# Plain float32 products in place of rounded high and low pairs, in the ternary and the last integer network

## The reference, cut to what matters

```
ternary:  a = silu((x @ w1.T) * w1_s) * ((x @ w2.T) * w2_s)      # 128 -> 512
          b = gelu((a @ h1.T) * h1_s)                            # 512 -> 512
          c = gelu((b @ h2.T) * h2_s)                            # 512 -> 512
          y = (c @ w3.T) * w3_s                                  # 512 -> 128
          with w1, w2, h1, h2, w3 in {-1, 0, 1}
integer:  y = (silu(x @ gate.T / 127) * (x @ up.T / 127)) @ down.T / 127   # 128 -> 384 -> 128
```

## Time and profile before

| what | value |
| --- | --- |
| median of 3 runs | 1074.12 us (1063.49 to 1074.72) |
| profiled execution, first to last instruction | 1068.8 us |
| PE busy | 941.6 us, 88% |
| DVE busy | 786.1 us, 74% |
| ACT busy | 692.7 us, 65% |
| POOL busy | 583.4 us, 55% |
| mean granted clock of TensorE | 0.893 of full speed |

### The profile page before, as it was taken

How to read it: one execution, slowest core, us unless ns; L and a number is a source line. 1 busy time by engine, 2 the same in 40 slices (tenths; PEclk the granted TensorE clock), 3 DMA queues, 4 the chain that set the end, 5 groups by cost and what they waited for, 6 DMA issues and landing times. The chain is left out here.

```text
span 1068.8 us, 19776 instructions
## 1 busy us (share of the span) xinstructions
PE 941.6 (88%) x6850; PEld 690.5 (65%) x6850; DVE 786.1 (74%) x1468; ACT 692.7 (65%) x1920; POOL 583.4 (55%) x622
## 2 busy tenths in 40 slices
PE   8999999999999977787889988888988897897786
PEld 5888868676767336556656666666767676576544
DVE  4888875757466788987895898797698979733346
ACT  5767655555564476694695678786687776656454
POOL 0111044333333777777777667777777777776001
PEclk9999999999999678997795689897798978989899
DMA  7100001000000563533522423331331333131001
GB/s 237 40 21 2 2 1 45 1 1 1 1 1 12 124 146 92 132 81 80 130 59 61 101 61 73 73 70 41 73 73 38 73 73 74 47 105 40 1 1 39
DMA packets 58737, 62.07 MB, mean 58 GB/s; under 512 B 27760, under 2 KB 43152, under 8 KB 58256
## 3 DMA queue, kind: packets, MB, share of 16 engines
q1 hardware_dynamic: 42768, 36.41, 13.2%
q0 software_dynamic: 15872, 24.41, 10.1%
HBM read 52.65 MB, written 8.13 MB: 57 GB/s over the span
## 5 line engine op out<-in xcount | busy, mean ns | idle before, releaser
L791 POOL DMA_INDIRECT gathered_rows<-key_table,idx_T x496 | 482.5, 973 | 157.6 <-issue 146.6
L2382 DVE TENSOR_TENSOR turned_rows<-bank,rank_rope 96x512 f32<-96x512 f32 x128 | 87.3, 682 | 83.3 <-PE bank L1293 82.1
L1293 PE MATMUL bank<-ident,gathered_rows 128*96 128x128 f32 x512 | 92.6, 311 | 11.8 <-DVE turned_rows L2382 7.1
L2356 DVE SCALAR_TENSOR_TENSOR index_sums<-index_relu,iw,index_sums 128x512 f32<-128x512 f32 (+4 forms) x114 | 75.4, 661 | 33.4 <-ACT index_relu L1826 30.8
L832 PE MATMUL bank<-index_k_hi,index_q 128*128 128x512 f32 (+5 forms) x160 | 77.2, 485 | 19.3 <-DVE idx_T L2376 11.6
L1826 ACT ACTIVATE index_relu<-bank 128x512 f32<-128x512 f32 (+4 forms) x152 | 75.1, 507 | 24.0 <-PE bank L832 23.6
L1848 ACT ACTIVATE probs<-masked_scores,attn_columns 128x208 f32<-128x208 f32 x128 | 59.5, 465 | 31.3 <-DVE attn_columns L2392 26.7
L832 PE MATMUL bank<-probs_window,local_values 80*32 80x128 f32 x256 | 57.4, 311 | 24.7 <-ACT probs_picked L1864 23.1
L1293 PEld LDWEIGHTS bank<-ident,gathered_rows 128*96 128x96 f32 x512 | 66.0, 144 | 20.5 <-issue 11.4
L2364 DVE MAX8 top<-index_sums 128x8 f32<-128x320 f32 (+13 forms) x56 | 75.8, 1354 | 1.0
L2366 DVE FIND_INDEX8 idx_u<-top,index_sums 128x8 uint32<-128x320 f32 (+13 forms) x56 | 75.5, 1348 | 0.0
(11 more groups left out here) (295 smaller groups left out, 2430.4 us busy)
## 6 DMA issues: line engine op xcount, KB each, us to landing
queries_in<-q_rot SPq DMA_DIRECT2D x32, 256.0 KB
gathered_rows<-key_table,idx_T POOLq DMA_INDIRECT x496, 2.5
q_rot<-rotated SPq DMA_DIRECT2D x16, 256.0 KB, 3.3
queries_in<-q_lat SPq DMA_DIRECT2D x16, 256.0 KB
h<-in_h SPq DMA_DIRECT2D x2, 1024.0 KB, 7.9
q_lat<-q_latent_sb SPq DMA_DIRECT2D x8, 256.0 KB
local_values<-key_table SPq DMA_DIRECT2D x15, 80.0 KB
rope_tables<-in_cos_ql SPq DMA_DIRECT2D x4, 256.0 KB
```

Source lines behind the costliest of these rows:

```text
L791: pool.indirect_dma_start(out=G[i % 2][:, gather_place(i, q), :], out_offset=None, in_=key_table[0:index_width(i), :], in_offset=bass.Indi ...
L1293: last = pe.transpose(bank[2][0:ROW, j * P:(j + 1) * P], G[i % 2][:, gather_place(i, 4 * g + j), :], ident[:])
L2356: v.scalar_tensor_tensor(s_, r_, iw[:, h:h + 1], s_, ALU.mult, ALU.add).then_inc(i_used, 1)
L2382: v.tensor_tensor(GT[n % 2].rearrange("r (j p) -> r j p", j=4), bank[2][0:ROW, :].rearrange("r (j p) -> r j p", j=4), rank_rope[:].unsquee ...
```

## The change

Weights and activations of the three networks stay float32, and each product is one plain float32 product. The casts (POOL, ACT), the subtractions (DVE), the rounding of the weights on POOL and all semaphores for them go. ACT writes gelu, and DVE the gated product, directly into what the next product reads. The ternary weights are loaded where their rounded copies were. POOL has no work in the ternary networks any more: after its part of the first attention it goes on to the gathers, and all 16 of the first tile's come as soon as its indices are ready. SyncE no longer waits for the rounding before it loads the attention's weights, nor for the down products before the fixed rows of the first tile. In the last network the units take three pairs of banks in turn, (4, 5), (6, 7), (2, 3); unit 2 waits for the last variance to be read (`ln_sd`), unit j for the gated product of unit j - 3.

```diff
-        w1r, w2r, w3r = over("w1r", [HID], F32R), over("w2r", [HID], F32R), over("w3r", [NM, P], F32R)
-        h1r, h2r = over("h1r", [NM, HID], F32R), over("h2r", [NM, HID], F32R)
+        for n, shape in (("w1", [HID]), ("w2", [HID]), ("w3", [NM, P]), ("h1", [NM, HID]), ("h2", [NM, HID])):
+            LOAD[n] = over(n, shape)
...
+        def unit_banks(j):
+            at_ = (4, 6, 2)[j % 3]
+            return bank[at_], bank[at_ + 1]
...
 sync
-            sp.wait_ge(f_w, 5)
             for n, dst in (("WuqT", WuqT), ("WukT", WukT), ("WuvT", WuvT), ("Wout", Wout)):
...
             sp.wait_ge(t_store_k, STORES_K)
-            sp.wait_ge(f_down, 8)
...
 gpsimd
-                round_weights(2, (w1r, w1), (w2r, w2))
-                round_weights(3, (h1r, h1))
...
-            x_round(0)
-            for R in range(4):
-                ffn_half(R)
...
             def gather(i):
                 pool.wait_ge(i_idx, i + 1)
+                if i == 0:
+                    pool.wait_ge(t_store_k, STORES_K)
                 if i == 1:
                     pool.wait_ge(f_hid, 64)
-                for q in range(FIXED // QD + 4 * NM - EARLY_GATHER if i == 0 else 0, P // QD):
+                for q in range(FIXED // QD if i == 0 else 0, P // QD):
...
 tensor, ffn_up
-                    pe.wait_ge(f_x, 2 * R + u + 1)
+                    pe.wait_ge(ln_applied, LN0 + norm_index(k, r) + u + 1)
...
-                for o_, w in ((bank[2 * (j % 2)], w1r), (bank[2 * (j % 2) + 1], w2r)):
-                    mm(o_, w[:, m * P:m * P + P], x_hi[:, u, :], True, False)
-                    last = mm(o_, w[:, m * P:m * P + P], x_lo[:, u, :], False, True)
+                for o_, w in ((bank[2 * (j % 2)], w1), (bank[2 * (j % 2) + 1], w2)):
+                    last = mm(o_, w[:, m * P:m * P + P], chunk(xn, 2 * r + u))
...
 tensor, ffn_down
-                    pe.wait_ge(f_lo, 16 * R + 8 + u * NM + kk + 1)
-                    mm(bank[6 + u], w3r[:, kk, :], a_hi[:, u * NM + kk, :], kk == 0, False)
-                    last = mm(bank[6 + u], w3r[:, kk, :], a_lo[:, u * NM + kk, :], False, kk == NM - 1)
+                    pe.wait_ge(f_gelu, 16 * R + 8 + u * NM + kk + 1)
+                    last = mm(bank[6 + u], w3[:, kk, :], f_c[:, u * NM + kk, :], kk == 0, kk == NM - 1)
...
 tensor, hidden steps
-                        mm(bank[m], wt, hi[:, u * NM + kk, :], kk == 0, False)
-                        last = mm(bank[m], wt, lo[:, u * NM + kk, :], False, kk == NM - 1)
+                        last = mm(bank[m], w[:, kk, m * P:m * P + P], from_[:, u * NM + kk, :], kk == 0, kk == NM - 1)
...
 tensor, last network, unit
+                    elif j == 2:
+                        pe.wait_ge(ln_sd, LNF + NCH)
                     else:
-                        pe.wait_ge(n_gated, j - 1)
+                        pe.wait_ge(n_gated, j - 2)
...
-                    for o_, w in ((bank[4 + 2 * (j % 2)], gate_w), (bank[5 + 2 * (j % 2)], up_w)):
-                        mm(o_, w[:, m * P:m * P + P], x_hi[:, c % 2, :], True, False)
-                        last = mm(o_, w[:, m * P:m * P + P], x_lo[:, c % 2, :], False, True)
+                    for o_, w in zip(unit_banks(j), (gate_f, up_f)):
+                        last = mm(o_, w[:, m * P:m * P + P], chunk(xn, c))
...
 scalar
-                    if q >= 4:
-                        act.wait_ge(f_lo, 16 * R + q - 3)
-                    else:
-                        act.wait_ge(f_a, 8 * R + 5 + m)
-                    fn(f_full[:, q % 4, :], bank[m], ACT.Gelu, scale=sc[:, m:m + 1]).then_inc(f_gelu, 1)
+                    fn((f_b, f_c)[q // 8][:, q % 8, :], bank[m], ACT.Gelu, scale=sc[:, m:m + 1]).then_inc(f_gelu, 1)
...
 vector
-                    dve.wait_ge(f_gelu_hi, 16 * R + q + 1)
-                    v.tensor_tensor(lo[:, q % 8, :], f_full[:, q % 4, :], hi[:, q % 8, :], ALU.subtract).then_inc(f_lo, 1)
```

More of the change, by code:

```diff
@@ L173, in hybrid_kernel @@
         early_offset = (nc.sbuf_base + 31) // 32 * 32
-        h1, h2, w1, w2, w3, Wgk1, Wgk2 = (load(n) for n in ("h1", "h2", "w1", "w2", "w3", "Wgk1", "Wgk2"))
-        early_rest = sb("early_rest", [P, 2 * P])
+        early_rest = sb("early_rest", [P, 3 * T - 2 * P])
+        Wgk1, Wgk2 = load("Wgk1"), load("Wgk2")
         assert nc.sbuf_base - early_offset == 4 * 3 * T
@@ L235, in hybrid_kernel @@
         at[0] = LAYER
[L237 to L240, removed]
+        last_gated = over("last_gated", [2 * NM2, C])
+        at[0] = LAYER + P // QD * ROW
+        f_a, f_c, f_b = (over("ffn_" + n, [2 * NM, C]) for n in ("gated", "second", "first"))
+        SILU_AT = LAYER + 36 * C
+        at[0] = SILU_AT
         f_silu_sb, f_full = over("ffn_silu_out", [2, C]), over("ffn_full", [4, C])
@@ L389, in hybrid_kernel @@
                 "squared", "mean_sq", "rms", "rms_columns", "rms_turned", "normed", "projected_out"))
[L391 to L394, removed]
+        f_up, f_silu, f_gated, f_hid, f_gelu, f_down = (
+            sem("ffn_" + n) for n in ("up", "silu", "gated", "hidden", "gelu", "down"))
         ss_a, ss_u, ss_x, ss_y = (sem("ssm_" + n) for n in ("decay_ready", "inputs", "states", "outputs"))
@@ L426, in hybrid_kernel @@
                 "keys_x_values_added"))
-        (n_w, n_x_hi, n_x, n_up, n_silu, n_gated, n_gated_hi, n_a, n_down) = (
-            sem("int_" + n) for n in ("weights_ready", "x_hi", "x_split", "up", "silu", "gated", "gated_hi",
-                                      "gated_split", "down"))
+        n_w, n_up, n_silu, n_gated, n_down = (
+            sem("int_" + n) for n in ("weights_ready", "up", "silu", "gated", "down"))
         stored = sem("stored")
@@ L723, in gla @@
             def gla():
[L725 to L728, removed]
                 def out_gate(c):
@@ L752, in _ @@
             gla()
[L754 to L787, removed]
             def gather_rows(i, q):
@@ L1080, in ffn_half @@
                     stage, u, m = q // 8, q // 4 % 2, q % 4
-                    w, hi, lo = ((h1r, a_hi, a_lo), (h2r, b_hi, b_lo))[stage]
+                    w, from_ = ((h1, f_a), (h2, f_b))[stage]
                     if q < 4:
@@ L2008, in last_stages @@
                         act.wait_ge(n_gated, j - 1)
-                    fn(f_silu_sb[:, j % 2, :], bank[4 + 2 * (j % 2)], ACT.Silu, scale=INT_SCALE).then_inc(n_silu, 1)
-                    if j >= 1:
-                        gated_round(j - 1)
-                gated_round(NCH * NM2 - 1)
+                    fn(f_silu_sb[:, j % 2, :], unit_banks(j)[0], ACT.Silu, scale=INT_SCALE).then_inc(n_silu, 1)
             gla()
@@ L2167, in norm_apply @@
                     v.tensor_tensor(own, bank[4 + u], own, ALU.mult).then_inc(ln_applied, 1)
-            def x_rest(R, which=(0, 1)):
-                for u in which:
-                    c = 2 * (R % 2) + u
-                    dve.wait_ge(f_x_hi, 2 * R + u + 1)
-                    v.tensor_tensor(x_lo[:, u, :], chunk(xn, c), x_hi[:, u, :], ALU.subtract).then_inc(f_x, 1)
             def merge_weights():
@@ L2232, in ffn_half @@
                         early_setup(q)
-                    if q == 10 and R < 3:
-                        x_rest(R + 1)
                 add_down(R, 0)
```

98 lines of the change are left out of this document (20 added, 78 removed).

## The result

The kernel with plain products took a median of 1201.9 us (1196.6 to 1213.0 in four runs), the kernel before 1073.7 in the runs beside it: a ratio of **1.123, 95% interval 1.117 to 1.129**, 128 us slower. The prediction was 1208 us, +134. The profiled execution of the changed kernel took 1197.1 us, 1195.1 of it in the span.

What follows compares the result with a forecast made beforehand. TensorE was taken to bound the ternary stage: +130 us there, -2 behind it, 0 for the gathers' head start and +6 in the last network, +134 on 1074.1, gave 1208 us; own bounds 1196 to 1220, 8 in 10 within 1192 to 1221.

Steps and rivals of the forecast that it cites:

- Price of a product: Ternary stage: a plain product takes 0.86 us against 0.455 for a rounded pair, so 352 products add 142.6 us.
- Rival C: Ternary stage and last network: four passes make a plain product 0.91 us, 19 us more, 1227 us; chance 0.03.
- Waits and refills 18 to 5.5: Ternary stage: PE's non-streaming time, mostly in up units, falls as casts and subtractions go, -12.5 us.
- Moves of casts and loads at 0: First attention: dropping POOL's weight rounding and loading attention weights early are worth 0; rounding's bounds -1 to 0.
- Stage to last gather -2, with -6 to +2: Behind the ternary stage: full clock holds without the 1.88 us wait, but DVE's query rotation limits it to -2 us.
- The value 0 for the head start: Attention: gathers starting earlier gain nothing, since PE's side sets the pace until 620; bounds -13 and +3.
- the lower bound of -13: Attention: the head start's edge case, if PE's side also gains, through the clock.
- Rival A: Attention: faster PE side to 620, vanishing POOL waits and earlier gathers give back 12 us, 1196 us; chance 0.14.
- Last network +6: Last network: longer products fill PE's holes with a third pair of banks, +6 us, bounds +4.5 and +8.
- Sum: Whole kernel: 1202.8 us of span, carried to the median as 1074.1 + 134 = 1208 us; chance 0.68.
- B: Ternary stage or attention: TensorE's clock falls for 15 to 25 us more, giving 1216 to 1221 us; chance 0.10.
- D: Accumulating groups: a plain product costs no more than a pair, 0.455 us, so not slower, 1057 us; chance 0.01.

Runs made afterwards that it cites:

- the kernel with two passes: Kernel before with gelu and gated product writing the rounded tile, both passes reading it, low halves left out: 0.993 of before, ternary stage 215.2 us.
- the held ones: Changed kernel with 20 small copies on GpSimd ahead of tile 2's gathers: 1207.3 us against 1200.5 without them; 1206.0 in the first session.
- The kernel with early gathers: Kernel before with the last half pass's last five casts moved from GpSimd to ScalarE: 0.994 on the 1314 us chip, 0.9957 (1068.1 us) on another.

## Why the prediction was right, point by point

- **Price of a product.** 0.86 us, and 352 x 0.405 = 142.6: held. Rival C's 0.91 us would have made it 3.64 us for four; the rows show 3.44.
- **Waits and refills 18 to 5.5.** The stage came out at 349.35 us, forecast 349.65. With 352 x 0.86 and the same 41 us of other products it has 5 to 6 of waits and refills. The step held; the kernel with two passes splits it: 4.5 us for the copies behind the up units and gelus, and the other 8 for what is left, the cover of the loop in the main. The 0.1 us allowed for each up unit is there too: silus of the first half pass are 1.72 to 1.83 us apart (once 2.61, with small products between). DVE, ACT and POOL left a third or more of every half pass free, not a fifth, which changes nothing.
- **Moves of casts and loads at 0.** Held: the stage starts 0.2 us later (135.19 for 134.97).
- **Stage to last gather -2, with -6 to +2.** This is the step that failed: the profile has -9.8, and the means of three profiles each -8.0. The value 0 for the head start was wrong: holding it back cost 6.8 us in the median and 4.6 by the profiles. I had taken GpSimd's last long wait for PE at 620 to mean that PE's side sets the pace until there and a head start ends in waits. For the first 190 us that holds, since TensorE reaches tile 5 no sooner in the changed kernels than in the held ones. But PE's side then gains itself: the 37 us at half clock between tiles 5 and 6 go when the gathers start 2.7 us behind the stage, which is 7 to 10 us. That is the lower bound of -13 ("if PE's side also gains, through the clock"), which I had as an edge and not as the value. Rival A named PE's side as well, but for other reasons: GpSimd's waits did not vanish (8.1, 15.0 and 10.8 us against 8.9 to 12.4), and the clock right behind the stage, at which I had put the -2, gave nothing by tile 2. The half-clock stretch there did go, but another came 25 us later (0.59).
- **Last network +6.** +6.0 in all five profiles that have it, worked forward from unit to unit: unit 3 waited 0.64 us (forecast 0.8). The last product ended 32.7 us behind the end of the third variance product (1158.68 to 1191.35, which is the start of the last three products at 1188.77 and 3 x 0.86), forecast 32.6.
- **Sum.** +134 forecast, +128 measured: the difference is the attention's. 1201.9 us lies as near to rival A's 1196 as to the forecast, so it is the stage and the last network, right to 0.3 us, that bear the forecast out, and not the total.
- **Rivals B, C and D** didn't come: no stretch below full clock in the stage, no hidden product at 0.91, and none near 0.50. That a plain product might hide under other work was never near, since PE had 1.5 us of idling left in 349.

## What to carry to other kernels

Where TensorE bounds a stage, a plain float32 product against a rounded pair is decided by TensorE's distances from start to start; the casts and subtractions between the layers paid 4.5 us here where the products cost 142.6. Separate what a removed copy gives from what a longer product hides, because only the first is to be had without the price. And when two engines are nearly even over a long stage, don't put a head start at none from one long wait: hold it back in a kernel of its own, and compare both engines' progress and the granted clock tile by tile, in more than one profile. Look for the head start by itself too, since here five casts moved to another engine made the kernel 0.4% faster (0.1 to 0.8).

## What was not expected of the hardware

- The kernel before took 1314 us on one chip and 1072 on others. The kernel with early gathers was profiled on both, with spans of 1299.7 and 1065.2 us: the ternary stage is the same (218.5 and 218.6), the distance is 821.0 and 627.9, and from the last gather to the last addition it is 121.7 and 80.9. GpSimd's waits behind tile 2's first gather sum to 224 us there (8.9 on the other chip), with the first of 22.2 us. The profiles don't name the cause.
- In seven of ten profiles TensorE had the half clock for 37 us on end in the attention while it was nearly always busy: 36.44 of 37.50 us in the row of the kernel before. The same work took 7 to 10 us less in the three others.
- A table load of 1.28 us twice around two Ln and Exp kept ScalarE 5.2 us from its gelus, and the 3.0 us that PE then waited were followed by rounded passes 0.43 us apart instead of 0.2276: a stall was paid a second time by the clock. So it was with the wait of 2.36 us in the last network with two pairs of banks, but not with that of 0.64 us with three.
